# Local attention: inverse norms of queries and keys as one power on GpSimd in place of a chain on ScalarE and VectorE

## The reference, cut to what matters

```
def l2norm(t):
    return t / jnp.maximum(jnp.linalg.norm(t, axis=-1, keepdims=True), 1e-12)
...
qkv = x @ Wqkv
q, k, v = jnp.split(qkv, 3, -1)
...
q = l2norm(q) * qs
k = l2norm(k) * ksc
...
q = q * cos * scale + rotate_half(q) * sin * scale
inv = 1.0 / scale
k = k * cos * inv + rotate_half(k) * sin * inv
out = local_attention(q, k, v)
```

## Time and profile before

| | us |
|---|---|
| time, median of 3 runs | 5003.74 (5001.85 to 5009.4) |
| the profiled execution: time | 5000.08 |
| the profiled execution: span | 4998.3 |
| mean granted TensorE clock, share of full speed | 0.794 |
| PE busy | 3727.4 (75%) |
| DVE busy | 3243.7 (65%) |
| ACT busy | 2552.9 (51%) |
| POOL busy | 2185.2 (44%) |

### The profile page before, as it was taken

How to read it: one execution, slowest core, us unless ns; L and a number is a source line. 1 busy time by engine, 2 the same in 40 slices (tenths; PEclk the granted TensorE clock), 3 DMA queues, 4 the chain that set the end, 5 groups by cost and what they waited for, 6 DMA issues and landing times. The chain is left out here.

```text
span 4998.3 us, 82970 instructions
## 1 busy us (share of the span) xinstructions
PE 3727.4 (75%) x28548; PEld 2323.5 (46%) x28548; DVE 3243.7 (65%) x8012; ACT 2552.9 (51%) x7024; POOL 2185.2 (44%) x1599
## 2 busy tenths in 40 slices
PE   5288788798798798797868667855555655587997
PEld 2166466366466465464353442333333333354664
DVE  5777476476575575574372644499999999832343
ACT  2199498498597596695212221233433333235443
POOL 0177276275374473572221200177777777600000
PEclk8599899899899899899586778755555555567998
DMA  0011111111111011111000000000000000000000
GB/s 18 28 44 47 36 47 47 35 47 45 39 47 56 27 47 50 33 48 54 0 1 10 1 26 0 0 1 1 1 1 1 1 1 1 1 8 23 1 1 9
DMA packets 48674, 110.18 MB, mean 22 GB/s; under 512 B 8945, under 2 KB 9201, under 8 KB 46705
## 3 DMA queue, kind: packets, MB, share of 16 engines
q1 hardware_dynamic: 48240, 104.66, 6.7%
HBM read 31.23 MB, written 1.05 MB: 6 GB/s over the span
## 5 line engine op out<-in xcount | busy, mean ns | idle before, releaser
L1090 POOL TENSOR_TENSOR slabs<-slabs 128x512 f32<-128x512 f32 x768 | 951.8, 1270 | 380.2 <-DVE slabs L957 323.2
L1651 PE MATMUL psum<-constants,slabs 128*128 128x128 f32 x1264 | 327.4, 416 | 470.5 <-POOL slabs L1851 469.9
L1848 POOL TENSOR_SCALAR slabs<-slabs 128x512 f32<-128x512 f32 x256 | 501.7, 1960 | 335.8 <-DVE slabs L1804 335.8
L860 ACT ACTIVATE slabs<-slabs 128x96 f32<-128x96 f32 x1536 | 553.0, 361 | 18.8 <-PE psum L671 13.3
L1713 ACT ACTIVATE slabs<-slabs 128x512 f32<-128x512 f32 x316 | 211.9, 720 | 620.3 <-DVE slabs L1825 620.3
L624 PE MATMUL psum<-slabs 128*128 128x512 f32 x768 | 409.5, 660 | 128.8 <-DVE slabs L957 63.2
L1079 POOL TENSOR_TENSOR slabs<-slabs 128x768 f32<-128x768 f32 x192 | 282.0, 1469 | 490.1 <-DVE slabs L932 490.1
L1651 PEld LDWEIGHTS psum<-constants,slabs 128*128 128x128 f32 x1264 | 217.5, 209 | 582.1 <-POOL slabs L1851 543.9
L1804 DVE MAX8 slabs<-annex 128x8 f32<-128x272 f32 x1024 | 394.4, 424 | 0.0
L942 DVE TENSOR_REDUCE slabs<-slabs 128x16 f32<-128x1024 f32 x192 | 234.2, 1220 | 225.3 <-ACT slabs L811 225.2
L671 PE MATMUL psum<-constants,slabs 128*96 128x128 f32 x1536 | 245.1, 283 | 153.7 <-ACT slabs L853 150.3
(11 more groups left out here) (396 smaller groups left out, 8398.9 us busy)
## 6 DMA issues: line engine op xcount, KB each, us to landing
slabs<-slabs SPq DMA_DIRECT2D x192, 192.0 KB, 2.5
slabs<-slabs SPq DMA_DIRECT2D x192, 128.0 KB, 2.5
slabs<-F1A SPq DMA_DIRECT2D x7, 2176.0 KB, 9.3
slabs<-slabs SPq DMA_DIRECT2D x144, 64.0 KB, 2.1
slabs<-F1F SPq DMA_DIRECT2D x6, 580.5 KB, 4.6
slabs<-S SPq DMA_DIRECT2D x4, 645.0 KB, 5.7
weights<-M SPq DMA_DIRECT2D x1, 2184.0 KB, 9.4
weights<-R SPq DMA_DIRECT2D x2, 1079.5 KB, 5.2
```

What stands on the lines that cost most here:

```text
L860: last = nc.scalar.activation(probs[:, n, :], masked[:, n, :], ACT.Exp, bias=shifts[:, n:n + 1], accum_out=denom[:, n:n + 1])
L1090: nc.gpsimd.tensor_tensor(out[:, at, :], normed[u % 2][:, at, :], table, ALU.mult).then_inc(rope_done, 1)
L1651: last = nc.tensor.transpose(ps[:, 4 + n % 2, k * P:k * P + P], probs[j][:, k * P:k * P + P], m.ident)
L1848: nc.gpsimd.tensor_scalar(kept[n % 2], scores[slot], tops[:, slot, TOPK - 1:TOPK], None, ALU.is_ge).then_inc(kept_ready, 1)
```

## The change

The four activations of `root_of_sum` and the two VectorE corrections `measure` and `refine` go. VectorE clamps the sums from below at 1e-24 (`clamp`, one operation on 128x16), and GpSimd raises them to the power -0.5 (`invert_norms`, one operation on 128x16 with the exponent from a constant column), which gives the inverse norms. GpSimd does this for unit i+1 between the query products and the key products of unit i. `normalise` now waits for GpSimd. The constant factor that the Newton step left, until now taken back by the rotation tables, leaves them. The cut diff:

```diff
@@ local_layer: tiles and steps
-    logs, grown, root = (small[:, 16 + 16 * i:32 + 16 * i] for i in range(3))
+    clamped, root = (small[:, 16 + 16 * i:32 + 16 * i] for i in range(2))
...
-    ROOT_STEPS, MAX_STEPS = 3, 2
+    ROOT_STEPS, MAX_STEPS = 2, 2
@@ scalar
-            def root_of_sum(u):
-                act.wait_ge(root_step, ROOT_STEPS * u + 1)
-                nc.scalar.activation(logs, sums, ACT.Relu, scale=LIFT, bias=m.tiny[:, 2:3]).then_inc(logged, 1)
-                act.wait_ge(logged, 3 * u + 1)
-                nc.scalar.activation(logs, logs, ACT.Ln, bias=m.tiny[:, 3:4]).then_inc(logged, 1)
-                act.wait_ge(logged, 3 * u + 2)
-                nc.scalar.activation(root, logs, ACT.Exp, scale=-0.5).then_inc(logged, 1)
-                act.wait_ge(logged, 3 * u + 3)
-                nc.scalar.activation(logs, root, ACT.Square).then_inc(rooted, 1)
-
...
-                if i < UNITS:
-                    root_of_sum(i)
@@ vector
-            def measure(u):
+            def clamp(u):
+                dve.wait_ge(root_step, ROOT_STEPS * u + 1)
+                if u >= 1:
+                    dve.wait_ge(rooted, u)
+                nc.vector.tensor_scalar(clamped, sums, LEAST, None, ALU.max).then_inc(root_step, 1)
+
+            def normalise(u):
                 dve.wait_ge(rooted, u + 1)
-                nc.vector.scalar_tensor_tensor(out=grown, in0=sums, scalar=LEAST, in1=logs, op0=ALU.max, op1=ALU.mult).then_inc(root_step, 1)
-
-            def refine(u):
-                dve.wait_ge(root_step, ROOT_STEPS * u + 2)
-                nc.vector.scalar_tensor_tensor(out=root, in0=grown, scalar=-3.0 / LIFT, in1=root, op0=ALU.add, op1=ALU.mult).then_inc(root_step, 1)
-
-            def normalise(u):
-                dve.wait_ge(root_step, ROOT_STEPS * u + 3)
                 if u >= 2:
                     dve.wait_ge(rope_done, 4 * (u - 1))
...
                 if i < UNITS:
                     sum_squares(i)
-                    measure(i)
+                    clamp(i)
...
                 if i < UNITS:
-                    refine(i)
                     normalise(i)
@@ gpsimd
+            def invert_norms(u):
+                pool.wait_ge(root_step, ROOT_STEPS * u + 2)
+                if u >= 1:
+                    pool.wait_ge(unit_normed, u)
+                nc.gpsimd.tensor_tensor(root, clamped, m.minus_half.broadcast_to([P, 16]), ALU.pow).then_inc(rooted, 1)
+
-            def rope(u):
+            def rope(u, side):
...
             for i in range(UNITS + 3):
+                if i == 0:
+                    invert_norms(0)
                 if i >= 3:
                     finish_probs(i - 3)
                 if i < UNITS:
-                    rope(i)
+                    rope(i, 0)
+                if i + 1 < UNITS:
+                    invert_norms(i + 1)
+                if i < UNITS:
+                    rope(i, 1)
@@ rotary_tables
-    return f(1024 * -0.5 * LIFT) * kinds.reshape(4, P, 4, HD1).transpose(1, 0, 2, 3).reshape(P, -1)
+    return kinds.reshape(4, P, 4, HD1).transpose(1, 0, 2, 3).reshape(P, -1)
```

More of the change, by code:

```diff
@@ L270, in __init__ @@
         self.tiny, self.ones_row = constant("tiny"), constant("ones_row", 1)
+        self.minus_half = self.tiny[:, 2:3]
     def slab(self, i, n=1):
@@ L478 @@
 UNITS = 2 * (TOK // P)
-LIFT, LEAST = 2.0 ** 20, 1e-24
+LEAST = 1e-24
 QK_SCALE = 8.0
@@ L586, in local_layer @@
     with phase(nc, "forward_loaded qk_product qT_product kT_product v_product score_product pT_product pv_product out_product "
-                   "squared logged rooted kT_copied qT_copied v_copied exp_done pT_copied context_copied "
+                   "squared rooted kT_copied qT_copied v_copied exp_done pT_copied context_copied "
                    "root_step unit_normed k_roped q_roped masked_step inverted resid_done "
@@ L591, in local_layer @@
             block, forward_loaded, qk_product, qT_product, kT_product, v_product, score_product, pT_product, pv_product, out_product,
-            squared, logged, rooted, kT_copied, qT_copied, v_copied, exp_done, pT_copied, context_copied,
+            squared, rooted, kT_copied, qT_copied, v_copied, exp_done, pT_copied, context_copied,
             root_step, unit_normed, k_roped, q_roped, masked_step, inverted, resid_done,
@@ L1079, in finish_probs @@
                 nc.gpsimd.tensor_tensor(probs, probs, scale, ALU.mult).then_inc(probs_ready, 1)
-            def rope(u):
+            def invert_norms(u):
[4 more added lines that the diff above has]
+            def rope(u, side):
                 b, t, half = place(u)
                 pool.wait_ge(unit_normed, u + 1)
[L1084 to L1090, removed]
+                at = slice(8 * side, 8 * side + 8)
+                if u >= 1:
+                    pool.wait_ge(q_roped if side == 0 else k_roped, u)
+                for k, out in ((0, cosines), (1, sines)):
+                    table = tables[:, t, 2 * side + k:2 * side + k + 1, :].broadcast_to([P, 8, HD1])
+                    nc.gpsimd.tensor_tensor(out[:, at, :], normed[u % 2][:, at, :], table, ALU.mult).then_inc(rope_done, 1)
             for i in range(UNITS + 3):
+                if i == 0:
+                    invert_norms(0)
                 if i >= 3:
@@ L2497, in constants @@
     tiny[:, 1] = 1e-6
-    tiny[:, 2], tiny[:, 3] = -LIFT * LEAST, LIFT * LEAST
+    tiny[:, 2] = -0.5
     return pack(CONST_PARTS, {
```

## The result

| | before | after |
|---|---|---|
| time, median us | 5004.85 (4 runs) | 5432.15 (5430.0 to 5657.97, 4 runs) |
| ratio of the times | | 1.0852, 95% interval 1.0834 to 1.087 |
| the profiled execution: time | 5000.08 | 5433.95 |
| mean granted TensorE clock | 0.794 | 0.784 |
| one power on 128x16 | | 2.89 |

The change makes the kernel 8.5% slower; I had 5035 us and a range up to 5150. The longest of the four runs was a disturbed one and isn't in the ratio.

A forecast was written before the change was run, and what follows sets the result against it. Loop A was taken as the bound, loop B almost as long and the bound after the change. 192X - 90 us at X = 0.63 gave +31 on 5003.7, some 5035 us; range 4945 to 5150.

The forecast's parts named there:

- X: Time one power on 128x16 holds GpSimd: guessed 0.63 us, bounded between 0.10 and 1.96 us.
- 192X - 90 us: Total time change over six layers of 32 units, from X = 0.2 up; break-even at X = 0.47 us.
- Loop B: GpSimd's scaling and rotation products, VectorE's additions and reciprocal, next scaling: 8.33 us per unit, 7.98 alone.
- Loop B becomes 7.98 + X: The power in GpSimd's queue delays everything behind it, so the unit lasts 7.98 us plus X.
- Loop A: Normalise, projection, square, sum, ScalarE's four activations, first correction, maxima, next normalise: claimed closed without slack, the bound at 8.32 us.
- its last 2.70 us: Loop A from the sum's end to normalise: activations, corrections, waits and maxima (0.94), to be replaced by clamp, maxima and power.
- What ScalarE saves ... lies off loop B: Dropping the activations saves ScalarE some 1.16 us per unit, which was said not to shorten loop B.
- no engine is full: In the 2080 us of local attention: TensorE busy 1735, ScalarE 1590, VectorE 1329, GpSimd 1227 us.
- The place of the power: Between GpSimd's query and key products, costing nothing beyond X: clamp done about 11.1, queue there only at 12.25.
- X - 1.3: Time change of each of a layer's first four units, where the sum's end to normalise took 1.62 us.
- still near 0.94: TensorE's granted clock in the local attention was to stay at its level before the change.
- Rival 4: GpSimd loads code for the power in each layer: about 6 us each, 36 us in six layers; chance 1 in 20.

The follow-up runs named there:

- e7: After, with single powers of 1 to 128 columns and multiplies of 4, 16 and 128 run once on GpSimd ahead of the layers: 5471.7 us.
- e2: After, with the power on 8 columns instead of 16, its result serving queries and keys alike: 5187.78 us, ratio to before 1.0362.
- e3: Before, with a 128x16 power that nobody reads put between GpSimd's query and key products: 5436.87 us, ratio 1.086.
- e5: Before, with the maxima of unit i-3 moved ahead of the first correction of unit i on VectorE: 5010.38 us, ratio 1.001.
- e10: Before, with the logarithm and rough root in PSUM, so each correction has one operand there, and two waits added: 5003.96 us, ratio 1.0014.
- e11: e10 with the maxima ahead of the corrections: 4989.69 us, ratio to before 0.9985.
- e13: Before without Newton step, ScalarE taking Ln of the sums over 64 and Exp (4923.21 us), plus two unread ScalarE activations: 4997.38 us, ratio 0.9981.
- e1: After, with GpSimd's power replaced by a multiply of the same operands in the same place: 4927.64 us, ratio to before 0.9843.
- e8: e5 with both VectorE corrections replaced by operations with one SBUF input, the Newton correction left out: 5008.71 us, ratio to before 1.0006.

## Why the prediction was wrong

- **X, the size of the power: the step that failed.** I took 0.63 us as sixteen multiplies per element, and 1.96, the costliest row of the engine, as the upper bound. It is 2.89; per element that is 65 multiplies at the rate of the earlier trace rows (e7). No row of before held a power, and the costliest row of other operations bounds nothing. (The row of 512 elements there, L1260, is an addition; the rotation's products of the earlier trace rows, which are multiplies, take the same 1.24 us.) The 5150 at which the range ended was X = 1.23, so the range left out even my own upper bound.
- **"192X - 90 us": right.** At X = 2.89 it gives +465; the profiled executions differ by 434. Loop B without the power is 7.89 and not 7.98 us, because the reciprocal starts a little before the additions' end (-15 us in 168 units), and the mean unit of before is 8.40 and not the 8.33 of the two that I followed (-12).
- **"Loop B becomes 7.98 + X": right in mechanism.** 7.89 + X holds in after, e2 and e3, and a power that nobody reads costs as much.
- **"Loop A, now the bound", "each starts as the one before ends": wrong.** Its first link was open in my own rows: `normalise` ends at 14.79 and the projection starts at 14.99, 0.20 us later, where 0.06 is what that link takes when it binds. The loop that closes runs from ScalarE's activations over its copies and TensorE's scores. With the maxima out of loop A (e5), with its holds gone (e10) and with both (e11) the unit stays; with two activations that nobody reads it comes back (e13). I had also read its last 2.70 us as plain durations; of the 0.45 and 0.26 us of `refine`, all but some 0.16 (e10) was GpSimd's hold.
- **"What ScalarE saves ... lies off loop B", and "no engine is full": the first is true, and yet what ScalarE saves is the source of e1's gain.** I had divided 1590 by 2080 us over a stage that holds six feed-forward parts as well; 131.71 of 140 inside a layer says otherwise. The sum came out nearly right because I had measured the old unit and not derived it. At a small X it was short: e1, at 0.22 us, gained 78 us where 192X - 90 gives 48; with the 15 and 12 us of the second point above it gives 75. Its mean unit is 8.16, so 168 x 0.24 = 40 us lie in the units and the rest at the ends of the layers.
- **The place of the power, "the clamp is ready": right** in 168 of 192 units. The first unit of the first layer goes from the end of the sum to `normalise` in 231.33 - 228.09 = 3.24 us, against 1.62 in the earlier trace rows: X - 1.3 more, as written.
- **TensorE's clock "still near 0.94": wrong.** It is 0.89 in the stage, in which TensorE was busy 1901 of 2506 us and not 1735 of 2080. A projection took 1.98 us in the median in place of 1.88, off the bound.
- **Rival 4, code loaded per layer: no run shows that it costs anything.** Ahead of each layer GpSimd has two MODIFY_POOL_CONFIG instructions in the trace, in before (12 for the six layers, the first at 221.6) as in after (12, at 221.9). In after each layer's first power comes 6.3 to 7.4 us later, 0.08 us after its clamp, and takes 2.89 to 2.92 us. In e7 no wait hides such a time, and the first power starts 0.06 us after them.

The Trainium skill (GPSIMD Engine Reference, section 3.1), by whose two-input rate the power would have taken 0.2 us, fits the multiply in the same place (0.22) and misses the power more than tenfold.

## What to carry to other kernels

Price an operation that no row shows by running it alone, and if that can't be done, don't bound it by rows of other operations of the engine: per column the power took as long as 65 multiplies here, and 1.96 us for the dearest other row said nothing of its 2.89. Before a chain of waits is called the bound, take busy plus waits of each engine inside one steady period, not over a stage: an engine whose only waits are short and for its own result stands in the bound, and its small instructions count, up to the next bound (here 0.57 us of them cost 0.32 us in the mean unit). A loop is closed only where every link starts as the one before ends: compare each hand-over with the same one in a run where it does bind, since 0.2 us in place of 0.06 is slack. And undo or pad one link of each loop that you suspect.

## What the runs showed of the hardware

- A power on GpSimd on 128 partitions took 0.71 us for one column, 1.63 for 8, 2.89 for 16 and 20.7 for 128, which from 16 on is 0.159 us for each further column; a multiply took 0.21 at 16 and 0.40 at 128.
- VectorE's Newton corrections and clamp from SBUF to SBUF on 128x16, with one input or two, may last until the GpSimd instruction that runs beside them ends, up to 1.2 us (e5, e8) or 1.3 (after) in place of 0.17; with one operand in PSUM the corrections took 0.16 to 0.17 us in all 192 units (e10). `normalise`, which reads PSUM, took 1.22 us throughout, and the sums, a reduction from SBUF to SBUF, 1.21 to 1.22 beside the same products.
- An activation of 128x16 is 0.21 to 0.31 us. Two more of them in each unit, 0.57 us of ScalarE's queue, cost 66 us in 192 units (e13), 0.34 us per unit.
